# Second attention with its transpositions set among the attend products, and the down product's tiles in another order

## The chip, the cores and the metric

The kernel runs on one core of one Trainium2 chip. The metric is the device time of one execution in microseconds, as the median of the runs. Engines are named by the profile: PE is TensorE (matmuls and transpositions; PEld its weight loads), DVE is VectorE, ACT is ScalarE, POOL is GpSimd, SP is SyncE, which here only issues DMAs.

## What is computed

Two layers with residuals on x of shape (2, 512, 512): attention with 32 heads of 128, a gated feed-forward network, a second attention with 32 heads of 16, and a mixture of low-rank experts. The change lies at the end of the feed-forward network and in the second attention:

```python
def _L0_ffn_ref(x, ...):
    hidden = jax.nn.silu(x_flat @ gate_w.T) * (x_flat @ up_w.T)
    return hidden @ down_w.T                       # FF = 1792, H = 512
def _L1_attn_ref(x, w_qkv, b_qkv, w_out, b_out):   # N_HEADS = 32, hd = 16
    q, k, v = jnp.split(jnp.einsum('bsd,od->bso', x, w_qkv) + b_qkv, 3, axis=-1)
    scores = jnp.einsum('bqhd,bkhd->bhqk', q, k) * scale
    scores = scores + alibi[None, :, None, :]      # slope of the head * position
    scores = jnp.where(causal, scores, -1e9)
    attn = jax.nn.softmax(scores, axis=-1)
    out = jnp.einsum('bhqk,bkhd->bqhd', attn, v).reshape(B, S, D)
    return jnp.einsum('bsd,od->bso', out, w_out) + b_out
x = x + ffn(layernorm(x)); x = x + attn(layernorm(x)); x = x + experts(layernorm(x))
```

## The kernel before

x lies in eight tiles of 128 rows; tiles 0 to 3 are one batch, 4 to 7 the other. A product of two f32 operands is made of three matmuls on their rounded high and low halves (helper `product`, lines 64 to 66), each 128 x 128 by up to 512 columns. Every engine has its own hand-written program; they meet at semaphores only.

**Feed-forward, second half.** The down product of tiles 4 to 7 (`second_sequence`) sums 14 chunks of the hidden layer (`FC` = 14, three matmuls each) per tile in one PSUM bank. TensorE's order is: tile 4 whole; tile 5's first seven chunks; the transpositions of batch 0's normalised tiles (`norm.turn(0)`); tile 5's rest; the projection of the second attention's first query; tile 6's first half; the projection of keys; tile 7's first half; tile 6's rest; tile 7's rest; the projection of values. Each chunk of tile 7 counts `chunk_free`, from which GpSimd knows that memory of the hidden layer may be overwritten with the second attention's operands. VectorE scales each finished tile, adds it to x and takes its moments (`add_out`).

**Second attention.** Heads are taken in 4 chunks; a chunk is 8 heads for each of two batches, 16 units (batch, head), 64 units in all. Query and keys are projected for a whole chunk and batch, split in high and low halves (`split_operand`, VectorE, behind a rounding on ScalarE, `round_operand`), written out by SyncE (`a_spill_q`, `a_spill_k`) and read back by GpSimd (`read_back`) stacked by head in `stacked_q` and `stacked_k`, together with a block of slopes (`in_slope`), so that one matmul gives a score with its position term. A pick matrix and zeros are put in `stacked_q` first (`prepare`).

One step of TensorE (`step(c, s)`, line 1896) works on three units at once: it scores unit s + 3 (`score`, four matmuls of 128, 256, 384 and 512 columns into two banks, line 1828), turns the probabilities of unit s + 1 (`turn`, ten 128 x 128 transpositions in three groups of 4, 3 and 3, one PSUM bank each, line 1841), and attends unit s (`attend`, line 1853: four matmuls with the high halves of the turned probabilities, four with the low ones, 512, 384, 256 and 128 columns, all summed in one bank). Behind them stand, by the step's number, the turning of four gathered units, parts of the output product, and halves of the next projections (`project`), or `spread`.

VectorE per step: adds a projection's bias, masks the four scores of a unit and takes their maxima (`mask`, line 1992), takes the low half of the three turned groups (`split_turned`, line 2000). ScalarE per step (line 2156): exponentials of score tiles 0 and 1, casts of the three turned groups to the high half (`round_turned`, line 2132; its semaphore is `turned_hi`), in some steps one pass over values, spread values or the attended result, exponentials 2 and 3 (line 2123), the copy of the attended bank (`gather`, line 2140; `attend_read`), in some steps `round_operand`. The first attend of a unit waits for `attend_read` and for the low halves (`turned_split`); the first transposition waits for the four exponentials of its unit (`exp_done`).

At the start `step(-1, 13)` scores unit 0 behind the values' projection, once the pick has landed; then the values are spread and batch 1's normalised tiles turned (`norm.turn(1)`), and the loop begins at `step(-1, 14)`. Step 0 is the first with all three parts.

GpSimd's queue holds `read_back` with its waits, the splitting of weights and the addition of the output bias; SyncE's queue the loads of weights, the spills, and, behind the last spill, the loads of the experts' weights (`moe.fetch_down`, four of 512 KB).

## Time and profile before

| | |
|---|---|
| median of 3 runs | 1504.5 us (1502.46 to 1506.17) |
| the profiled execution | 1505.23 us, its span 1503.2 us |
| PE, PEld busy, share of the span | 95%, 80% |
| DVE, ACT, POOL busy | 67%, 57%, 37% |
| second attention, step 0 to step 52 | 1078.5 to 1334.2 us |

The table's shares are averages over stages with different limits. The prediction reads the stretch of the second attention by itself, then the order of time of an engine, in which each row is a run of like instructions with its start and duration; matmuls overlap, so a run's rate is read from the distance of starts. In brackets stands idle time ahead of a row and what ended it.

### The profile page before, as it was taken

The page shows a single profiled execution, that of the slowest core. Times are in us where ns is not written, and L with a number is a line of the kernel's source. Part 1 is how long each engine was busy: PE and PEld are TensorE (multiplying, and loading weights), DVE is VectorE, ACT ScalarE, POOL GpSimd, SP SyncE. Part 2 cuts the span into 40 slices and gives each one's busy share as a digit, 9 for nine tenths or more (in the row PEclk, how much of TensorE's full clock was granted, in tenths as well). Part 3 has the DMA queues.
Part 4 walks back from the last instruction along what each step waited for, and adds up shares of the span by engine and source line. Part 5 has one row for each costly group of instructions (what it writes and reads, how often), then busy time and mean ns, then how long its engine had stood idle before and what let it go on. Part 6 is the DMA issues. An engine that isn't in the chain of part 4 may idle for free.

```text
span 1503.2 us, 25443 instructions
## 1 busy us (share of the span) xinstructions
PE 1433.1 (95%) x7696; PEld 1195.1 (80%) x7696; DVE 1009.5 (67%) x2538; ACT 857.5 (57%) x2184; POOL 555.7 (37%) x484
## 2 busy tenths in 40 slices
PE   5899999999999999999988999999789999988999
PEld 4788888888888888888867888888567777776787
DVE  7776667766777667666656333344688889889742
ACT  2676566655566556665653332220589989988310
POOL 5474464644645456454240000023161314116500
PEclk9999999999999999999999999999899999999999
DMA  4010110100100001000021111114434435461000
GB/s 171 8 50 15 29 43 21 28 21 28 35 21 28 28 28 35 14 28 7 1 71 43 63 60 45 42 36 78 75 84 76 96 69 102 78 144 57 1 22 35
DMA packets 37517, 71.97 MB, mean 48 GB/s; under 512 B 4993, under 2 KB 5377, under 8 KB 36865
## 3 DMA queue, kind: packets, MB, share of 16 engines
q1 hardware_dynamic: 29664, 55.35, 11.8%
q0 software_dynamic: 7776, 15.73, 7.1%
q8 instruction: 33, 0.54, 0.2%
q14 instruction: 44, 0.35, 0.1%
HBM read 60.58 MB, written 10.49 MB: 47 GB/s over the span
## 4 chain that ended last, share of the span: by engine, by line
PE 80%; ACT 6%; DVE 6%; issue 4%; DMA 2%; POOL 1%; DVEq 0%; ACTq 0%; SPq 0%; POOLq 0%
PE ps_up L66 9%; PE ps_up L65 9%; PE ps_up L64 9%; PE ps_gate L64 8%; PE ps_gate L66 8%; PE ps_gate L65 8%; PE ps_out L64 5%; PE ps_out L66 5%; PE ps_out L65 5%; PE ps_out L556 4%; PE ps_up L1853 2%; ACT a_probs L2123 2%; PE ps_out L1841 2%; PE ps_gate L1828 2%; ACT a_probsT_hi L2132 2%
## 5 line engine op out<-in xcount | busy, mean ns | idle before, releaser
L822 ACT ACTIVATE a_probs<-a_probs,a_least 128x512 f32<-128x512 f32 (+3 forms) x256 | 143.0, 560 | 162.2 <-DVE a_least L683 157.2
L405 POOL TENSOR_TENSOR a_rotated<-a_by_cos,a_by_sin 128x512 f32<-128x512 f32 x80 | 103.7, 1296 | 224.9 <-DVE a_by_sin L706 222.7
L691 DVE TENSOR_TENSOR a_probsT_lo<-ps_out,a_probsT_hi 128x512 fp32r<-128x512 f32 (+3 forms) x256 | 118.5, 484 | 67.9 <-ACT a_probsT_hi L830 66.7
L830 ACT CAST a_probsT_hi<-ps_out 128x512 fp32r<-128x512 f32 (+3 forms) x256 | 101.5, 427 | 92.4 <-PE ps_out L556 91.6
L2123 ACT ACTIVATE a_probs<-a_probs,a_least 128x128 f32<-128x128 f32 (+3 forms) x256 | 142.2, 560 | 3.4 <-issue 1.6
L1992 DVE CUSTOM_DVE_ANT_0 a_probs<-ps_gate,a_causal 128x128 f32<-128x128 f32 (+3 forms) x256 | 117.1, 486 | 33.6 <-PE ps_gate L1828 20.7
L882 ACT ACTIVATE a_probs<-a_probs,a_inverse 128x128 f32<-128x128 f32 (+3 forms) x256 | 123.1, 553 | 9.6 <-DVE a_inverse L724 8.6
L415 POOL TENSOR_TENSOR a_query_lo<-a_rotated,a_query_hi 128x512 fp32r<-128x512 f32 x64 | 82.7, 1292 | 107.8 <-ACT a_query_hi L842 107.8
L683 DVE CUSTOM_DVE_ANT_0 a_probs<-ps_out,a_causal 128x512 f32<-128x512 f32 (+2 forms) x192 | 101.2, 551 | 29.6 <-PE ps_out L66 29.6
L64 PE MATMUL ps_up<-a_wo_hi,a_attended_hi 128*128 128x512 f32 x278 | 113.4, 408 | 2.3 <-issue 1.4
L64 PE MATMUL ps_gate<-xT_hi,a_wq_hi 128*128 128x512 f32 x256 | 108.9, 425 | 1.6 <-DVE a_values_lo L719 1.6
L2000 DVE TENSOR_TENSOR a_probsT_lo<-ps_out,a_probsT_hi 128x384 fp32r<-128x384 f32 (+1 forms) x192 | 108.8, 595 | 1.4 <-ACT a_probsT_hi L2132 1.2
L66 PE MATMUL ps_up<-a_wo_hi,a_attended_lo 128*128 128x512 f32 x278 | 108.9, 392 | 0.0
L65 PE MATMUL ps_up<-a_wo_lo,a_attended_hi 128*128 128x512 f32 x278 | 108.7, 391 | 0.0
L556 PE MATMUL ps_out<-ident,a_probs 128*128 128x128 f32 x640 | 102.5, 275 | 2.5 <-ACT a_probs L882 2.5
L66 PE MATMUL ps_gate<-xT_hi,a_wq_lo 128*128 128x512 f32 x256 | 100.6, 393 | 0.0
L65 PE MATMUL ps_gate<-xT_lo,a_wq_hi 128*128 128x512 f32 x256 | 100.1, 391 | 0.0
L2132 ACT CAST a_probsT_hi<-ps_out 128x384 fp32r<-128x384 f32 (+1 forms) x192 | 85.9, 512 | 22.6 <-PE ps_out L1841 22.0
L1828 PE MATMUL ps_gate<-a_stacked_k,a_stacked_q 128*128 128x128 f32 (+3 forms) x256 | 76.0, 374 | 21.9 <-DVE a_least L1992 13.4
L1841 PE MATMUL ps_out<-ident,a_probs 128*128 128x128 f32 x640 | 91.5, 274 | 5.2 <-ACT a_probs L2123 4.3
L713 DVE TENSOR_TENSOR x<-ps_up,x 128x512 f32<-128x512 f32 x64 | 44.2, 691 | 77.3 <-PE ps_up L66 77.3
L556 PEld LDWEIGHTS ps_out<-ident,a_probs 128*128 128x128 f32 x640 | 80.6, 142 | 13.8 <-ACT a_probs L882 3.0
(279 smaller groups left out, 4082.5 us busy)
## 6 DMA issues: line engine op xcount, KB each, us to landing
a_raw<-in_wq SPq DMA_DIRECT2D x36, 256.0 KB, 2.7
a_raw<-in_wo SPq DMA_DIRECT2D x36, 256.0 KB, 2.6
a_stacked_q<-a_spill_q POOLq DMA_DIRECT2D x48, 128.0 KB, 4.5
a_stacked_k<-a_spill_k POOLq DMA_DIRECT2D x24, 256.0 KB, 4.6
f_raw<-in_gate SPq DMA_DIRECT2D x14, 256.0 KB, 2.7
f_raw<-in_up SPq DMA_DIRECT2D x14, 256.0 KB, 2.9
f_raw<-in_down SPq DMA_DIRECT2D x14, 256.0 KB, 3.5
a_raw<-in_wk SPq DMA_DIRECT2D x12, 256.0 KB, 2.8
```

The costliest lines, as they stand in the source:

```text
L64: nc.tensor.matmul(out, left[0], right[0], start=start, stop=False)
L65: nc.tensor.matmul(out, left[0], right[1], start=False, stop=False)
L66: return nc.tensor.matmul(out, left[1], right[0], start=False, stop=stop)
L556: last = nc.tensor.transpose(ps_turn[:, t % 2, (i - t) * P:(i - t + 1) * P], probs[:, u % 2, at:at + P], m.ident[:])
L691: nc.vector.tensor_tensor(probsT[1][:, t % 2, 0:w], ps_turn[:, t % 2, 0:w], probsT[0][:, t % 2, 0:w].bitcast(F32), ALU.subtract).then_inc( ...
L822: nc.scalar.activation(tile, tile, ACT.Exp, bias=least[:, slot, i:i + 1], scale=-1.0, accum_out=total[:, slot, i:i + 1]).then_inc(exp_done, 1)
L882: nc.scalar.activation(tile, tile, ACT.Copy, scale=inverse[:, slot, i:i + 1]).then_inc(probs_ready, 1)
L1841: last = nc.tensor.transpose(ps_turn[:, t, to:to + P], probs[:, u % 4, at:at + P], m.ident[:])
L1992: nc.vector.tensor_tensor_reduce(out=probs[:, u % 4, at:at + w], in0=ps_score[:, i % 2, 0:w], in1=causal[:, SEQ - w:SEQ], scale=-float(HD1 ...
L2000: nc.vector.tensor_tensor(probsT[1][:, u % 2, at], ps_turn[:, t, 0:TURNED_WIDTH[t]], probsT[0][:, u % 2, at].bitcast(F32), ALU.subtract).t ...
L2123: nc.scalar.activation(tile, tile, ACT.Exp, bias=least[:, u % 4, i:i + 1], scale=-1.0, accum_out=total[:, u // 4 % 2, i, u % 4:u % 4 + 1]) ...
L2132: nc.scalar.copy(probsT[0][:, u % 2, at], ps_turn[:, t, 0:TURNED_WIDTH[t]]).then_inc(turned_hi, 1)
```

## The change

It has five parts. (1) In `step` the ten transpositions, eight attends and four scores no longer stand in blocks but one by one among each other; `attend` waits for `turned_hi` ahead of the four high products and for `turned_split` ahead of the four low ones. (2) The down product's order: first halves of tiles 4, 5 and 6, `norm.turn(0)`, first half of tile 7, then the rests with the query's and keys' projections between; the first unit is scored in the middle of tile 7's second half; values' projection, `spread` and `norm.turn(1)` follow it. (3) VectorE adds tiles 4 and 5 behind the keys' split, masks unit 0, then adds tiles 6 and 7; the query's `split_operand` in the last two steps ahead of step 0 comes one step later. (4) GpSimd issues the slopes ahead of the wait for the spilled keys (`fetch_slope`) instead of behind the keys. (5) SyncE waits for all keys read back (`stacked_k_in`) before it loads the experts' first weights. `least` and `total` move to another place in memory.

```diff
-    least = at("least", [P, 4, QT], DOWN_S_AT + 1056)
-    total = at("total", [P, 2, QT, 4], DOWN_S_AT + 1120)
+    least = at("least", [P, 4, QT], SMALL_AT + 256)
+    total = at("total", [P, 2, QT, 4], SMALL_AT + 320)
...
     def read_back(pool, c, s):
...
         else:
+            if not (isinstance(c, int) and c < 0):
+                fetch_slope(pool, c, s)
+            wait(pool, keys_out, 2 * 16 * (p + 1))
+            pool.sem_inc(wait_passed_pool, 1)
             for place, part in enumerate((0, 1, 0)):
...
-            pool.dma_start(stacked_k[96:P, b]..., dram["slope"][c if s < 8 else c + 1]).then_inc(stacked_k_in, 16)
+    def fetch_slope(pool, c, s):
+        pool.sem_inc(wait_passed_pool, 1)
+        pool.dma_start(stacked_k[96:P, batch_of(s)]..., dram["slope"][c if s < 8 else c + 1]).then_inc(stacked_k_in, 16)
...
         sp.wait_ge(keys_out, 2 * 16 * 2 * CHUNKS1)
+        sp.wait_ge(stacked_k_in, 16 * DMAS_K * 2 * CHUNKS1)
         moe.fetch_down(sp, (0, 1))
...
         prepare(0)
+        pool.wait_ge(ffn.chunk_free, 5)
+        fetch_slope(pool, -1, 8)
         read_back(pool, -1, 6)
-        pool.wait_ge(ffn.chunk_free, 5)
         read_back(pool, -1, 8)
...
         def attend(attending, part, k):
...
+            if k == 0:
+                if part == 0:
+                    if j == 0:
+                        wait(pe, side_read, side_count(cu, 3) if b else side_count(cu - 1, 11))
+                    wait(pe, attend_read, n)
+                    wait(pe, turned_hi, 3 * n + 3)
+                else:
+                    wait(pe, turned_split, 3 * n + 3)
...
         ffn.tensor(pe, bank_read, reads)
-        ffn.second_sequence(pe, 4, range(FC))
-        ffn.second_sequence(pe, 5, range(half))
+        for t in (4, 5, 6):
+            ffn.second_sequence(pe, t, range(half))
         norm.turn(pe, 0)
-        ffn.second_sequence(pe, 5, range(half, FC))
+        ffn.second_sequence(pe, 7, range(half))
         norm.ready(pe, 0)
         project(-1, 6, [0, 1])
-        ffn.second_sequence(pe, 6, range(half))
+        ffn.second_sequence(pe, 4, range(half, half + 3))
         project(-1, 8, [0, 1])
-        ffn.second_sequence(pe, 7, range(half))
+        ffn.second_sequence(pe, 4, range(half + 3, FC))
+        ffn.second_sequence(pe, 5, range(half, FC))
         ffn.second_sequence(pe, 6, range(half, FC))
-        ffn.second_sequence(pe, 7, range(half, FC))
+        pe.wait_ge(pick_in[0], 16)
+        pe.wait_ge(ffn.out_scaled, 6)
+        score((0, 0), 0)
+        score((0, 0), 1)
+        ffn.second_sequence(pe, 7, range(half, half + 4))
+        score((0, 0), 2)
+        score((0, 0), 3)
+        ffn.second_sequence(pe, 7, range(half + 4, FC))
         project(-1, 10, [0, 1])
+        spread(-1, 11)
+        norm.turn(pe, 1)

         def step(c, s):
             scoring, turning, attending = unit(c, s, 3), unit(c, s, 1), unit(c, s, 0)
-            turn 0; turn 1; score 0, 1; turn 2; attend 0; score 2, 3; attend 1
+            turn(turning, 0, [0, 1])
+            attend(attending, 0, 0)
+            score(scoring, 0)
+            attend(attending, 0, 1)
+            score(scoring, 1)
+            turn(turning, 0, [2])
+            attend(attending, 0, 2)
+            turn(turning, 0, [3])
+            attend(attending, 0, 3)
+            attend(attending, 1, 0)
+            turn(turning, 1, [0])
+            attend(attending, 1, 1)
+            turn(turning, 1, [1])
+            attend(attending, 1, 2)
+            turn(turning, 1, [2])
+            attend(attending, 1, 3)
+            turn(turning, 2, [0, 1, 2])
+            score(scoring, 2)
+            score(scoring, 3)
...
-        pe.wait_ge(pick_in[0], 16)
-        pe.wait_ge(ffn.out_scaled, 6)
-        step(-1, 13)
-        spread(-1, 11)
-        norm.turn(pe, 1)
         pe.wait_ge(pick_in[1], 16)
         each_chunk(pe, step)
...
     VectorE:
-        ffn.add_out(dve, 4)
-        ffn.add_out(dve, 5)
...
-            if side1 in ("query", "keys") and isinstance(c1, int) and c1 < 0:
+            if side1 in ("query", "keys") and isinstance(c1, int) and c1 < 0 and s1 < STEPS1 - 2:
                 split_operand(c1, s1)
-            if side2 in ("query", "keys") and not (isinstance(c2, int) and c2 < 0):
+            if side2 in ("query", "keys") and not (isinstance(c2, int) and c2 < 0 and s2 < STEPS1 - 2):
                 split_operand(c2, s2)
...
         step(-1, 9)
+        ffn.add_out(dve, 4)
+        ffn.add_out(dve, 5)
+        dve.wait_ge(causal_in, 16)
+        dve.wait_ge(ffn.chunk_free, 9)
+        step(-1, 13)
         ffn.add_out(dve, 6)
         ffn.add_out(dve, 7)
         norm.shift(dve, 1)
-        dve.wait_ge(causal_in, 16)
-        step(-1, 13)
```

On TensorE, one step before (`L1841` is `turn`, `L1828` `score`, `L1853` `attend`) begins so:

```order
L1841 MATMUL ps_out<-ident,a_probs 128x128 [waits a1_turned_split,a1_exp_done]
L1841 MATMUL ps_out<-ident,a_probs 128x128 x3
L1841 MATMUL ps_out<-ident,a_probs 128x128 [waits a1_turned_split]
L1841 MATMUL ps_out<-ident,a_probs 128x128 x2
L1828 MATMUL ps_gate<-a_stacked_k,a_stacked_q 128x128 [waits a1_score_masked]
L1828 MATMUL ps_gate<-a_stacked_k,a_stacked_q 128x256 [waits a1_score_masked]
L1841 MATMUL ps_out<-ident,a_probs 128x128 [waits a1_turned_split]
L1841 MATMUL ps_out<-ident,a_probs 128x128 x2
L1853 MATMUL ps_up<-a_probsT_hi,a_values 32x512 [waits a1_turned_split,a1_attend_read]
L1853 MATMUL ps_up<-a_probsT_hi,a_values 32x384
L1853 MATMUL ps_up<-a_probsT_hi,a_values 32x256
L1853 MATMUL ps_up<-a_probsT_hi,a_values 32x128
```

Behind these stand scores 2 and 3 and the four attends with the low half. The same step of the changed kernel (`L1857` is `turn`, `L1875` `attend`, `L1839` `score`):

```order
L1857 MATMUL ps_out<-ident,a_probs 128x128 [waits a1_turned_split,a1_exp_done]
L1857 MATMUL ps_out<-ident,a_probs 128x128
L1875 MATMUL ps_up<-a_probsT_hi,a_values 32x512 [waits a1_turned_hi,a1_attend_read]
L1839 MATMUL ps_gate<-a_stacked_k,a_stacked_q 128x128 [waits a1_score_masked]
L1875 MATMUL ps_up<-a_probsT_hi,a_values 32x384
L1839 MATMUL ps_gate<-a_stacked_k,a_stacked_q 128x256 [waits a1_score_masked]
L1857 MATMUL ps_out<-ident,a_probs 128x128
L1875 MATMUL ps_up<-a_probsT_hi,a_values 32x256
L1857 MATMUL ps_out<-ident,a_probs 128x128
L1875 MATMUL ps_up<-a_probsT_hi,a_values 32x128
L1875 MATMUL ps_up<-a_probsT_lo,a_values 32x512 [waits a1_turned_split]
L1857 MATMUL ps_out<-ident,a_probs 128x128 [waits a1_turned_split]
```

The first attend moves from behind ten transpositions to behind two, with another semaphore; eight transpositions come behind it. What follows is attend and transposition by turns, the third group of transpositions in a row, and scores 2 and 3 last.

On TensorE ahead of the loop, the first unit's scores before stand behind the values' projection (`a_wv`) and ahead of `spread` and `norm.turn(1)` (`L179`):

```order
L65 MATMUL ps_out<-xT_lo,a_wv_hi 128x512
L66 MATMUL ps_out<-xT_hi,a_wv_lo 128x512
L1828 MATMUL ps_gate<-a_stacked_k,a_stacked_q 128x128 [waits a1_stacked_q_in,a1_stacked_k_in,f0_out_scaled,a1_pick_in0]
L1828 MATMUL ps_gate<-a_stacked_k,a_stacked_q 128x256
L1828 MATMUL ps_gate<-a_stacked_k,a_stacked_q 128x384 [waits a1_score_masked]
L1828 MATMUL ps_gate<-a_stacked_k,a_stacked_q 128x512 [waits a1_score_masked]
L1793 MATMUL ps_out<-ident,a_values_turned 128x128 [waits a1_side_read]
L1793 MATMUL ps_out<-ident,a_values_turned 128x128 x3
L179 MATMUL ps_up<-ident,f_hidden 128x128 [waits ln_lo_done,ln_normal_done]
```

In the changed kernel they stand within the down product (`f_chunks`), the first two ahead of the first four of tile 7's last seven chunks:

```order
L65 MATMUL ps_up<-f_chunks 128x512
L66 MATMUL ps_up<-f_chunks 128x512
L1839 MATMUL ps_gate<-a_stacked_k,a_stacked_q 128x128 [waits a1_stacked_q_in,a1_stacked_k_in,f0_out_scaled,a1_pick_in0]
L1839 MATMUL ps_gate<-a_stacked_k,a_stacked_q 128x256
L64 MATMUL ps_up<-f_chunks 128x512
L65 MATMUL ps_up<-f_chunks 128x512
L66 MATMUL ps_up<-f_chunks 128x512
```

The first scores pass 33 products, 21 of tile 7 and 12 of the values' projection, and the scores of 384 and 512 columns stand four chunks behind the first two.

On SyncE behind the last spill of keys (`L1659`), before:

```order
L1659 DMA a_spill_k<-a_keys_hi 128x512 [waits a1_operand_split,a1_stacked_k_in]
L1659 DMA a_spill_k<-a_keys_lo 128x512
L1666 DMA a_raw<-in_wo 128x512 [waits a1_piece_split]
L1205 DMA moe_down_raw_5140<-in_down 128x1024 [waits a1_keys_out,a1_query_out]
L1205 DMA moe_down_raw_5141<-in_down 128x1024
L1205 DMA moe_down_raw_5142<-in_down 128x1024 [waits a1_side_made]
L1205 DMA moe_down_raw_5143<-in_down 128x1024
L1209 DMA moe_router_raw<-in_router 128x256
```

And in the changed kernel (`L1665` is the spill):

```order
L1665 DMA a_spill_k<-a_keys_hi 128x512 [waits a1_operand_split,a1_stacked_k_in]
L1665 DMA a_spill_k<-a_keys_lo 128x512
L1672 DMA a_raw<-in_wo 128x512 [waits a1_piece_split]
L1205 DMA moe_down_raw_5140<-in_down 128x1024 [waits a1_stacked_k_in,a1_keys_out,a1_query_out]
L1205 DMA moe_down_raw_5141<-in_down 128x1024
L1205 DMA moe_down_raw_5142<-in_down 128x1024 [waits a1_side_made]
L1205 DMA moe_down_raw_5143<-in_down 128x1024
L1209 DMA moe_router_raw<-in_router 128x256
```

The four loads of `in_down` keep their place, but the first waits for one thing more, the keys read back by GpSimd, and so do all behind it.

## Rows read from the trace of the kernel before

**Rows 1.** Windows, 52 steps: us, then PE, PEld, DVE, ACT, POOL busy

```profile
1078.70:1334.20 255.50, 244.35 (x1543) 193.64 (x1541) 225.63 (x669) 229.63 (x652) 76.07 (x102) 0.99 0.46 92
```

**Rows 2.** Timeline, PE before step 0: start, us, line, operation [idle <- releaser]

```profile
1057.91 0.47 PE L1828 MATMUL ps_gate<-a_stacked_k,a_stacked_q 128*128 128x128 f32 x2 [3.89 <-DMA a_stacked_k<-in_slope]
...
1061.54 1.97 PE L179 MATMUL ps_up<-ident,f_hidden 128*128 128x128 f32 x8 [0.77 <-DVE f_hidden L124]
...
1075.05 1.11 PE L1828 MATMUL ps_gate<-a_stacked_k,a_stacked_q 128*128 128x384 f32 x2 [3.32 <-DVE a_least L1992]
...
1078.52 1.11 PE L1841 MATMUL ps_out<-ident,a_probs 128*128 128x128 f32 x7
```

**Rows 3.** Timeline of PE, the last steps

```profile
1334.17 0.98 PE L1841 MATMUL ps_out<-ident,a_probs 128*128 128x128 f32 x7
...
1343.94 0.47 PE L1828 MATMUL ps_gate<-a_stacked_k,a_stacked_q 128*128 128x128 f32 x2 [3.93 <-issue]
...
1383.46 1.38 PE L1841 MATMUL ps_out<-ident,a_probs 128*128 128x128 f32 x10 [0.89 <-DVE a_probsT_lo L2000]
```

**Rows 4.** Timeline of PE, one step inside the attention

```profile
1207.16 0.93 PE L1841 MATMUL ps_out<-ident,a_probs 128*128 128x128 f32 x7
...
1208.16 0.49 PE L1841 MATMUL ps_out<-ident,a_probs 128*128 128x128 f32 x3
1208.41 0.83 PE L1853 MATMUL ps_up<-a_probsT_hi,a_values 128*32 128x512 f32 x4
...
1209.53 0.75 PE L1853 MATMUL ps_up<-a_probsT_lo,a_values 128*32 128x512 f32 x4
1210.11 0.44 PE L64 MATMUL ps_out<-xT_hi,a_wv_hi 128*128 128x512 f32 x1
```

**Rows 5.** Timeline of PE, first attention, a lone transposition

```profile
307.11 0.27 PE L556 MATMUL ps_out<-ident,a_probs 128*128 128x128 f32 x1
...
307.45 0.40 PE L65 MATMUL ps_gate<-xT_lo,a_wq_hi 128*128 128x512 f32 x1
307.68 0.39 PE L66 MATMUL ps_gate<-xT_hi,a_wq_lo 128*128 128x512 f32 x1
```

**Rows 6.** Timeline of ACT, end of one step

```profile
1353.38 1.32 ACT L2132 CAST a_probsT_hi<-ps_out 128x512 fp32r<-128x512 f32 x3
1354.59 0.63 ACT L2123 ACTIVATE a_probs<-a_probs,a_least 128x384 f32<-128x384 f32 x1
...
1355.20 0.71 ACT L2123 ACTIVATE a_probs<-a_probs,a_least 128x512 f32<-128x512 f32 x1
...
1356.03 0.57 ACT L2140 COPY a_gathered<-ps_up 32x512 f32<-32x512 f32 x1
```

**Rows 7.** Timeline of PE, start of the step behind it

```profile
1356.06 0.99 PE L1841 MATMUL ps_out<-ident,a_probs 128*128 128x128 f32 x7 [0.75 <-ACT a_probs L2123]
```

**Rows 8.** Timeline of ACT, a step with the result's rounding

```profile
1327.47 0.71 ACT L2145 ACTIVATE a_attended_hi<-ps_up,a_value_bias 128x512 fp32r<-128x512 f32 x1
1328.05 0.64 ACT L2123 ACTIVATE a_probs<-a_probs,a_least 128x384 f32<-128x384 f32 x1
```

**Rows 9.** Timeline of POOL ahead of step 0

```profile
1038.70 0.66 POOL L1748 DMA_DIRECT2D a_stacked_q<-in_pick  x1 [27.23 <-PE ps_up L66]
...
1047.39 1.62 POOL L1631 DMA_DIRECT2D a_stacked_k<-a_spill_k  x3 [0.80 <-issue]
```

**Rows 10.** Chain that ended last, before step 0: start, us, what

```profile
1039.65 6.94 DMA a_spill_k<-a_keys_lo
```

**Rows 11.** Page, part 6: DMA issues, count, KB each, us to landing

```profile
a_stacked_k<-a_spill_k POOLq DMA_DIRECT2D x24, 256.0 KB, 4.6
```

**Rows 12.** Timeline of DVE, one tile's addition and moments

```profile
1051.34 0.69 DVE L1078 TENSOR_TENSOR f_hidden<-ps_up,f_down_s 128x512 f32<-128x512 f32 x1 [2.40 <-PE ps_up L66]
...
1053.74 0.17 DVE L109 TENSOR_SCALAR ln_shifted<-moments 128x4 f32<-128x4 f32 x1
```

**Rows 13.** Timeline of SP, late in the attention

```profile
1329.10 2.14 SPq L1205 DMA_DIRECT2D moe_down_raw<-in_down  x4
```

More of the change, by code:

```diff
@@ L1829, in score, with turn @@
                              stacked_k[:, b, j // 2, 0:P * (i + 1)], start=True, stop=True).then_inc(score_made, 1)
[L1831 removed]
+        def turn(turning, t, blocks):
+            if not turning:
+                return
+            cu, u = turning
             n = STEPS1 * cu + u
[L1834 to L1842 removed]
@@ L1844, in attend @@
[L1844 to L1858 removed]
+            if 0 in blocks:
+                if t == 0:
+                    wait(pe, exp_done, 4 * n + 4)
+                wait(pe, turned_split, 3 * n - 2 + t)
@@ new lines, in turn, with attend @@
+            of_tile = [(k, i) for k in ((t,) if t < 2 else (2, 3)) for i in range(k, QT)]
+            for block in blocks:
+                k, i = of_tile[block]
+                at = SCORE_AT[i] + k * P
+                to = KEY_AT[k] - TURNED_AT[t] + (i - k) * P
+                mm = nc.tensor.transpose(ps_turn[:, t, to:to + P], probs[:, u % 4, at:at + P], m.ident[:])
+                if block == len(of_tile) - 1:
+                    mm.then_inc(turned, 1)
+        def attend(attending, part, k):
+            if not attending:
+                return
+            cu, u = attending
+            n, b, j = STEPS1 * cu + u, u // HPC, u % HPC
+            if k == 0:
[6 more added lines that the diff above has]
+                    wait(pe, turned_split, 3 * n + 3)
+            mm = nc.tensor.matmul(
+                ps_attend[0:2 * HD1, k * P:SEQ], values[:, b, k, j].rearrange("p h d -> p (h d)"),
+                probsT[part][:, u % 2, KEY_AT[k]:KEY_AT[k] + SEQ - k * P],
+                start=part == 0 and k == 0, stop=part == 1 and k == QT - 1)
+            if part == 1 and k == QT - 1:
+                mm.then_inc(attend_made, 1)
```

51 lines of the change are left out of this document (8 added, 43 removed).

## The prediction

> **What bounds the kernel now.** I read the stretches first, then the order of time of single steps, then the waits. In the second attention (52 steps, 1078.5 to 1334.2) TensorE is busy 244.35 of 255.5 us, ScalarE 229.63 and VectorE 225.63 [rows 1]: per step 4.70, 4.42 and 4.34 us against a step of 255.65 / 52 = 4.92 (first transposition at 1078.52 [rows 2] to that at 1334.17 [rows 3]). So TensorE's row sets the step, with the two others only 10% behind it; whatever lengthens a chain through ScalarE matters at once. Ahead of that stretch TensorE stands still for 3.89 us at the first score and 3.32 us at a later one [rows 2]; behind it, 3.93 us at 1343.94 [rows 3].
>
> **What interleaving changes on TensorE.** One step before: 7 transpositions, 2 scores, 3 transpositions, 4 attends, 2 scores, 4 attends, in 1210.11 - 1207.16 = 2.95 us [rows 4]. The four widths (512, 384, 256, 128 columns) take 1210.11 - 1209.53 = 0.58. A transposition costs 0.11: with one between wide products, the second product behind it comes 307.45 - 307.11 = 0.34 after it, of which 0.23 are the 512 columns (307.68 - 307.45) [rows 5]. So 10 x 0.11 + 3 x 0.58 = 2.84 (the scores have the four widths too): 0.11 per step is lost where a 128-column weight load follows a narrow product, and some 0.05 more at the first projection behind the last attend, an estimate from the same cause. In the new order no such load follows a narrow product but in the last three transpositions. TensorE's own gain is 0.11 to 0.16 us a step, 6 to 8 us over 52. A single transposition gets no cheaper: the lone one already costs what one in a row does (0.93 for seven, the last one's whole length included [rows 4]).
>
> The Trainium skill ("TensorE: Matmul & The Clock Gate", LDWEIGHTS) has a load of P columns take P / 1.2 ns, 107 ns for 128, and its section "Back-to-back issue gap" gives 128 moving columns some 56 ns. By that a row of transpositions is bound by its loads, and setting seven of ten among attends would hide 7 x 51 ns = 0.36 us a step. The trace speaks against it: 0.11 for a lone one [rows 5].
>
> **The chain that gets longer.** ScalarE's order is not touched: two exponentials, three casts of the turned tiles, exponentials 3 and 4, the copy `gather` of the attended bank, next step. The attend of the next unit writes the same bank, so it waits for that copy. Before, the attend stood 1208.41 - 1207.16 = 1.25 us behind the step's start, and the third group of transpositions ended 1208.16 + 0.49 - 1207.16 = 1.49 in [rows 4]. Now the first attend stands behind two transpositions (0.22), and from it to the last transposition stand 8 attends (1.16), 7 transpositions (0.77) and two scores (0.17): 2.10. From one first attend to the next: 2.10 + 0.27 (its own length [rows 5]) + 0.40 (a cast, a third of 1354.59 - 1353.38) + 0.61 (exponential 3, to 1355.20) + 0.83 (exponential 4, to the copy at 1356.03) + 0.57 (copy) [rows 6] + 0.05 to release = 4.83 us. The other branch, exponential 4 to the next transposition, is 1356.06 - 1355.20 = 0.86 [rows 6, 7] plus 0.22, under 1.45, so the copy ends last. This closes on itself: no step can be shorter, and long steps are not paid back by short ones. Before, the same links make 1.49 - 1.25 + 0.40 + 1.21 + 0.61 + 0.86 = 3.3, under every step.
>
> In three of eight steps one more ScalarE operation lies between the casts and exponential 3 (attended 1328.05 - 1327.47 = 0.58 [rows 8]; values and spread, one 512-column pass each, taken alike). So eight steps take at least 8 x 4.83 + 3 x 0.58 = 40.4, 5.05 each. Above that stands what the loop doesn't cover: the steps with the division and with both projection halves, where VectorE and TensorE are late anyway. TensorE's idle time in the stretch, 255.5 - 244.35 = 11.15 or 0.21 a step [rows 1], bounds it: 0 to 0.21. I take 0.13, nearer the upper end, since masks 3 and 4 and the third split now also wait behind the late casts on VectorE. Step 5.18, times 52 = 269.4, against 255.65: **+13.7 us** (5.05: +7; 5.26: +17.9).
>
> **The start.** Tile 7's first half now comes behind the normalised tile's transpositions, 22 groups of three products ahead of its old place: 66 x 0.23 = 15 us. So GpSimd's pick (0.5 MB) and memset, at 1038.70 before [rows 9], come at about 1023.6 and are gone when the keys are spilled; the keys' projection itself moves ahead by 12 products, 2.7 us. Before, the spill left at 1039.65 and took 6.94 beside the pick [rows 10]. After: it leaves at 1036.9 and lands in 4.6, as a read back of its kind does [rows 11], at best and 6.94 at worst; 0.3 to 0.8 to GpSimd's first read back, 1.1 to the issue of the third (1.62 for three [rows 9]), 4.6 to land: ready at 1048 to 1050. TensorE reaches the first score 33 products (7.6 us) before 1057.91 - 3.89 = 1054.0 [rows 2], at 1046.4. So the wait of 3.89 is down to 1.5 or a little more, and the unit's scores and masks lie beside tile 7's second half. Tile 7 ends near 1053; one tile's addition and moments take VectorE 1053.74 - 1051.34 = 2.40 [rows 12], so the first normalised tile is turned at about 1057 instead of 1061.54 [rows 2]: -4.5. The clock isn't lowered by such a wait: eight transpositions took 1.97 there [rows 2], seven take 0.93 in the loop [rows 4], which gives 1.3 on the sixteen (as if the second eight were partly hidden). Then the wait of 3.32 goes: the mask stood behind `split_operand`, which waited for ScalarE; it is now a step later. The two scores and six projection products behind that wait took 1078.52 - 1075.05 = 3.47 [rows 2], at 0.23 each 1.8: together -4.9. Sum **-11 us** up to step 0; bounds -8 (the wait of 1057.91 stays half) and -12.
>
> **The end.** The four `moe_down` loads went out at 1329.10 [rows 13], beside the last read back of keys, and TensorE waited 3.93 us for it [rows 3]. SyncE now waits for the keys. What is queued behind that wait are these loads and the router's, nothing else; they land some 7 us later than before, and their first user is GpSimd behind its split of `wo`. The slopes go ahead too, one transfer less behind the keys. That gives 3.9 back. But the last ten steps have few projections: they took 1383.46 - 1334.17 = 49.3 us with this wait [rows 3], 45.4 without, and at 4.83 plus two extra ScalarE passes they take 49.5 to 52. With the last attend behind the same copy: **+2.5 us** (0 to +4).
>
> Nothing: `least` and `total` elsewhere in memory; `turned_hi` for the first four attends (the split of the lower halves ends before their partners come); two more semaphore increments of GpSimd.
>
> **Sum.** 1505.2 (profiled) - 11 + 13.7 + 2.5 = 1510.4; the median of the three runs is 0.7 below the profiled one, so 1509.7, **1510**.
>
> **Rivals.** (a) The loop isn't binding, because some link is shorter than I read it: then TensorE's 0.16 a step comes through, and 1504.5 - 11 - 3.9 - 8 to -11 = about **1479**. For it: TensorE is still the busiest. Against it: ScalarE already held TensorE back at 1356.06, with 0.75 idle [rows 7]. (b) Transpositions are hidden by attends: 0.05 of the 0.11 of each of the seven goes, 0.36 a step, which shortens the loop by as much, to 4.47: 1504.5 - 11 - 3.9 with 52 x (4.92 - 4.7) = -11 and some -3 from the last ten steps, about **1475**. That is what the Trainium skill's rule quoted above would give. (c) The loop binds, but nothing is added to it: 5.05 a step, -11 + 7 + 1 = **1502**, no measurable difference. (d) Slower still: the keys land late. If spill and read back meet other transfers again they are there at 1051 to 1052, TensorE stands 5 us with tile 7 unfinished, and the clock falls as it did after the 3.89 us [rows 2]. Then the 21 down products run at about twice 0.23, which costs some 2 more; the start gains 4 instead of 11: **1517**. It decides from a landing later than about 1050.
>
> **Chances.** The forecast (1502 to 1518) 0.62, (a) 0.12, (b) 0.04, (c) 0.12, (d) 0.10. Within 0.3% (4.5 us, about what a measurement of this kernel can tell from no change) is 1500 to 1509. The forecast's case lies above it in some 0.38, in it in 0.21, below in 0.03. Slower 0.48, within 0.33, faster 0.19. The range takes both ends of the three terms: -12 + 7 + 0 = -5, -8 + 17.9 + 4 = +14, so 1499 to 1518; it leaves out (a) and (b).
>
> **What would show it.** Steps of 4.83 or more with TensorE idle before the first attend (ended by the copy) or the first transposition (by an exponential), ScalarE idle before the casts; steps of 5.3 to 5.5 where an extra pass lies on ScalarE. First transposition of step 0 near 1067.5, no wait over 2 us at the first score, none at 1340, the clock near 1 throughout. Wrong if short steps stay at 4.3 (then (a)), if 10 transpositions among attends add less than 0.9 us (then (b)), or if the first score waits more than 3 us (then (d)).

## The result and the profile after

| | before | changed |
|---|---|---|
| median of 3 runs | 1504.5 us (1502.46 to 1506.17) | 1521.2 us (1517.79 to 1521.76) |
| ratio of changed to before | | 1.0102 (95% interval 1.0075 to 1.0128) |
| span of the profiled execution | 1503.2 us | 1519.2 us |

The change makes the kernel 1% slower. The prediction had the sign, but said 1510 with an upper end of 1518, below what was measured. The spans differ by 16.0 us. I cut both traces at landmarks of TensorE that both programs have: the first transposition of batch 0's normalised tiles, that of batch 1's, the first transpositions of steps 0, 52 and 62, and the first transposition of the experts' normalised tiles. (This table and those below are worked out from the starts of those matmuls in each trace.)

| stretch, us | before | changed | difference | predicted |
|---|---|---|---|---|
| span's start to batch 0's transpositions | 1020.14 | 1023.02 | +2.9 | 0 |
| to batch 1's transpositions | 41.40 | 39.49 | -1.9 | -4.5 |
| to step 0 | 16.97 | 12.98 | -4.0 | -6.2 |
| 52 steps | 255.65 | 269.74 | +14.1 | +13.7 |
| steps 52 to 61 | 49.29 | 51.28 | +2.0 | +2.5 with the next row |
| last step to the experts' transpositions | 5.44 | 7.17 | +1.7 | |
| the experts | 114.27 | 115.47 | +1.2 | 0 |

The first row is no effect of the change: the down product's first matmul, which stands ahead of everything that was moved, already starts at 1008.60 instead of 1005.72. In the eleven other profiled kernels of this study the stretch took between 1018.9 and 1022.8 us.

The 52 steps as one window of the changed kernel (us, then busy time and instructions of PE, PEld, DVE, ACT, POOL, mean clock, DMA share, GB/s), to be read against [rows 1]:

```profile
1075.50:1345.20 269.70, 246.42 (x1541) 198.06 (x1541) 230.59 (x674) 237.18 (x657) 76.36 (x102) 1.00 0.47 88
```

TensorE is idle for 269.70 - 246.42 = 23.3 us there instead of 11.15. Of the 14.2 us by which the window is longer, 12.1 are idle time of TensorE and 2.1 busy time: its waits grew. The timeline of TensorE at two step starts (27 and 28) shows them:

```profile
1215.05 0.43 PE L1857 MATMUL ps_out<-ident,a_probs 128*128 128x128 f32 x2 [0.77 <-ACT a_probs L2155]
1215.64 0.42 PE L1875 MATMUL ps_up<-a_probsT_hi,a_values 128*32 128x512 f32 x1 [0.16 <-ACT a_gathered L2172]
...
1217.56 0.49 PE L1857 MATMUL ps_out<-ident,a_probs 128*128 128x128 f32 x3
...
1220.49 0.43 PE L1857 MATMUL ps_out<-ident,a_probs 128*128 128x128 f32 x2 [0.72 <-ACT a_probs L2155]
1221.09 0.41 PE L1875 MATMUL ps_up<-a_probsT_hi,a_values 128*32 128x512 f32 x1 [0.16 <-ACT a_gathered L2172]
...
1225.27 0.50 PE L64 MATMUL ps_out<-a_wo_hi,a_attended_hi 128*128 128x512 f32 x1 [0.94 <-DVE a_values L2094]
```

The same step on ScalarE, from one copy of the attended bank to the next:

```profile
1214.94 0.57 ACT L2172 COPY a_gathered<-ps_up 32x512 f32<-32x512 f32 x1
...
1216.79 0.59 ACT L2164 CAST a_probsT_hi<-ps_out 128x512 fp32r<-128x512 f32 x1 [0.26 <-PE ps_out L1857]
1217.70 0.87 ACT L2164 CAST a_probsT_hi<-ps_out 128x384 fp32r<-128x384 f32 x2 [0.33 <-PE ps_out L1857]
1218.46 0.59 ACT L2199 COPY a_values_turned<-ps_out 128x512 f32<-128x512 f32 x1
1218.94 0.63 ACT L2155 ACTIVATE a_probs<-a_probs,a_least 128x384 f32<-128x384 f32 x1
...
1219.56 0.71 ACT L2155 ACTIVATE a_probs<-a_probs,a_least 128x512 f32<-128x512 f32 x1
...
1220.38 0.57 ACT L2172 COPY a_gathered<-ps_up 32x512 f32<-32x512 f32 x1
```

This is the predicted loop, closed: copy at 1214.94, attend at 1215.64, last transpositions at 1217.56, casts to 1218.46, one more pass, exponentials 3 and 4, copy at 1220.38. It takes 5.44 us; the prediction had 4.83 + 0.58 = 5.41 for a step with an extra pass.

Ahead of step 0, TensorE of the changed kernel, against [rows 2]:

```profile
1051.75 0.47 PE L1839 MATMUL ps_gate<-a_stacked_k,a_stacked_q 128*128 128x128 f32 x2 [2.30 <-DMA a_stacked_k<-a_spill_k]
...
1062.02 0.66 PE L1801 MATMUL ps_out<-ident,a_values_turned 128*128 128x128 f32 x4 [1.85 <-ACT a_values_turned L2199]
1062.51 1.04 PE L179 MATMUL ps_up<-ident,f_hidden 128*128 128x128 f32 x8
...
1066.90 0.84 PE L1839 MATMUL ps_gate<-a_stacked_k,a_stacked_q 128*128 128x384 f32 x2 [2.25 <-DVE a_least L2021]
...
1068.23 0.63 PE L66 MATMUL ps_out<-xT_hi,a_wq_lo 128*128 128x512 f32 x1
1068.66 0.63 PE L64 MATMUL ps_out<-xT_hi,a_wq_hi 128*128 128x512 f32 x1
```

The wait of 3.89 us became 2.30, that of 3.32 us is gone, but waits of 1.85 and 2.25 us stand in between, where the kernel before waited 0.77 and 1.31. Behind them eight projection products come 0.43 us apart instead of 0.23.
### The profile page after: what moved, and what is told of

Read it like the earlier page. It is cut to its first block, busy times and chain, and to the rows that moved or that the text cites. A ratio compares the mean times of both kernels' runs of the same rounds, so it can differ in the third digit from the quotient of the medians.

```text
span 1519.2 us, 25451 instructions
## 1 busy us (share of the span) xinstructions
PE 1437.1 (95%) x7696; PEld 1201.7 (79%) x7696; DVE 1013.8 (67%) x2538; ACT 865.7 (57%) x2184; POOL 554.5 (37%) x484
## 4 chain that ended last, share of the span: by engine, by line
PE 82%; ACT 6%; DVE 5%; issue 2%; POOL 2%; DMA 2%; ACTq 0%; SPq 0%; DVEq 0%; POOLq 0%
PE ps_up L66 9%; PE ps_up L65 9%; PE ps_up L64 9%; PE ps_gate L64 8%; PE ps_gate L66 8%; PE ps_gate L65 8%; PE ps_up L1875 5%; PE ps_out L64 5%; PE ps_out L66 5%; PE ps_out L65 5%; PE ps_out L556 4%; PE ps_out L1857 4%; ACT a_probs L2155 2%; PE ps_gate L1839 2%; ACT a_gathered L2172 1%
## 5 line engine op out<-in xcount | busy, mean ns | idle before, releaser
L1857 PE MATMUL ps_out<-ident,a_probs 128*128 128x128 f32 x640 | 132.6, 276 | 20.1 <-ACT a_probs L2155 17.9
L2029 DVE TENSOR_TENSOR a_probsT_lo<-ps_out,a_probsT_hi 128x384 fp32r<-128x384 f32 (+1 forms) x192 | 112.7, 598 | 17.4 <-ACT a_probsT_hi L2164 12.6
L2164 ACT CAST a_probsT_hi<-ps_out 128x384 fp32r<-128x384 f32 (+1 forms) x192 | 93.0, 514 | 41.0 <-PE ps_out L1857 40.4
L1857 PEld LDWEIGHTS ps_out<-ident,a_probs 128*128 128x128 f32 x640 | 80.9, 142 | 36.4 <-ACT a_probs L2155 20.7
L556 PE MATMUL ps_out<-ident,a_probs 128*128 128x128 f32 x640 | 101.9, 274 | 2.5 <-ACT a_probs L882 2.5
L64 PE MATMUL ps_up<-a_probsT_hi,a_values_hi 128*128 128x512 f32 (+3 forms) x256 | 86.4, 337 | 4.8 <-DVE a_probsT_lo L691 4.7
```

The source lines that it names most:

```text
L64: nc.tensor.matmul(out, left[0], right[0], start=start, stop=False)
L556: last = nc.tensor.transpose(ps_turn[:, t % 2, (i - t) * P:(i - t + 1) * P], probs[:, u % 2, at:at + P], m.ident[:])
L1857: mm = nc.tensor.transpose(ps_turn[:, t, to:to + P], probs[:, u % 4, at:at + P], m.ident[:])
L2029: nc.vector.tensor_tensor(probsT[1][:, u % 2, at], ps_turn[:, t, 0:TURNED_WIDTH[t]], probsT[0][:, u % 2, at].bitcast(F32), ALU.subtract).t ...
```

## Experiments

Where a time is compared, it is with the kernel before on the same chip, run between (medians 1505.7 to 1506.5 us). Profiles give the place. Names used in the expectations: theory L is the loop above.

**Is it the step?** x1 takes the step's order back, x2 puts the new step alone into the kernel before.

```diff
 x1_old_step, against the changed kernel
-            turn(turning, 0, [0, 1])
-            attend(attending, 0, 0)
...
+            turn(turning, 0, [0, 1, 2, 3]); turn(turning, 1, [0, 1, 2])
+            score(scoring, 0); score(scoring, 1)
+            turn(turning, 2, [0, 1, 2])
+            for k in range(QT): attend(attending, 0, k)
+            score(scoring, 2); score(scoring, 3)
+            for k in range(QT): attend(attending, 1, k)
```

> The changed kernel with TensorE's step in the order of before (four and three transpositions, scores 0 and 1, three transpositions, four high attends, scores 2 and 3, four low attends); start, slopes and the late load of the experts' weights stay as changed. Theory L (the interleaved step is bound by a loop through ScalarE and the single attended bank): 52 steps take 255 to 257 us again instead of 269.7, the last ten some 45.5 instead of 51.3, and the tail loses its 3 us; with the start 6 us shorter than before that is 1494 to 1498. Rival S (the start or the later loads cost what was lost, not the step): 1515 to 1521.

Measured: 1500.73 us, ratio 0.9962 (0.9948 to 0.9976).

> The kernel before with the interleaved step alone. Theory L: 52 steps of 5.18, 269 to 271 us against 255.7 (+14), the wait of 3.9 us at the late load is still there but partly taken out of the same loop, the last ten steps 51 to 55: 1520 to 1525. Rival S: 1504 to 1508.

Measured: 1527.13 us, ratio 1.0145 (1.0126 to 1.0164), 2 us above what theory L gave and far from rival S. The 52 steps took 269.93 us as it said. The stretches ("to step 0" from batch 0's transpositions), with the mean length of a step by its place s in a round of eight (steps 8 to 51), for these and the next three kernels:

| | to step 0 | 52 steps | 52 to 61 | s=0 | 1 | 2 | 3 | 4 | 5 | 6 | 7 |
|---|---|---|---|---|---|---|---|---|---|---|---|
| before | 58.4 | 255.65 | 49.29 | 4.95 | 5.19 | 4.38 | 4.26 | 4.81 | 6.20 | 5.08 | 4.45 |
| changed | 52.5 | 269.74 | 51.28 | 5.24 | 5.02 | 5.18 | 5.42 | 5.61 | 5.56 | 4.91 | 4.60 |
| x1 | 52.9 | 260.08 | 45.78 | 4.92 | 5.20 | 4.39 | 4.25 | 4.81 | 6.38 | 5.08 | 4.43 |
| x2 | 57.8 | 269.93 | 53.55 | 5.24 | 5.02 | 5.18 | 5.42 | 5.61 | 5.57 | 4.91 | 4.60 |
| x3 | 52.9 | 260.69 | 47.96 | 5.18 | 4.90 | 4.69 | 5.00 | 5.19 | 5.61 | 4.97 | 4.27 |
| x4 | 54.2 | 266.65 | 48.98 | 5.24 | 5.06 | 4.90 | 5.22 | 5.60 | 5.58 | 4.91 | 4.33 |
| x5 | 52.8 | 251.95 | 44.92 | 4.95 | 5.16 | 4.39 | 4.25 | 4.81 | 6.26 | 5.09 | 4.43 |

The step is settled: x1 has the step lengths of before, x2 those of the changed kernel, and the 14 us go with it. It costs at s = 2, 3 and 4 (+0.80, +1.16, +0.80) and gives something back at s = 5 (-0.64).

x1 was expected at 1494 to 1498 and is slower. Its 52 steps took 260.08 instead of 255.65, and 3.0 of these 4.4 us are one step: step 5 takes 12.47 us, against 9.44 before and 6.89 in the changed kernel (0.8 more lie in step 6). GpSimd and VectorE of x1 there:

```profile
1093.79 9.92 POOL L1727 TENSOR_TENSOR x<-x,a_out_bias 128x512 f32<-128x512 f32 x8
...
1099.48 5.73 DVE L2041 TENSOR_TENSOR a_result<-a_summed,a_inverse 128x256 f32<-128x256 f32 x1
```

and what TensorE waits for:

```profile
1105.48 1.14 PE L1839 MATMUL ps_gate<-a_stacked_k,a_stacked_q 128*128 128x384 f32 x2 [5.66 <-DVE a_least L2013]
```

A product of 128 x 256 numbers that takes 0.42 us in most other places lasts 5.73. Whatever the start gained, this product ended at about the same time (1105.56 before, 1105.21 in x1), because GpSimd's eight additions of the output bias run where they ran: they stand in its queue behind the read back of keys (0, 0). That became theory G, tested below.

**Which links make the loop?** x3 shortens it on TensorE's side, x4 on ScalarE's.

```diff
 x3_third_group_early, against the changed kernel
             attend(attending, 0, 3)
-            attend(attending, 1, 0)
-            turn(turning, 1, [0])
...
+            turn(turning, 1, [0, 1, 2]); turn(turning, 2, [0, 1, 2])
+            for k in range(QT): attend(attending, 1, k)
             score(scoring, 2)
```

> The changed kernel with the six last transpositions in a row ahead of the four low attends: from the first attend to the last transposition 0.58 + 0.17 + 8 x 0.109 = 1.62 us instead of 2.10, so the loop is 4.35 instead of 4.83 us. Theory L: steps with no extra pass fall from 5.18 to some 4.8, the mean of 52 to 4.92 to 5.0, total 1505 to 1511. Rival T (a transposition or attend among the others costs TensorE more than one in a row): only three of seven are put back in a row, so at most three sevenths of the loss goes, 1515 or more.

Measured: 1506.74 us, ratio 1.0004 (0.9995 to 1.0013); the 52 steps took 260.69 us, 5.01 each, and 4.97 in steps 8 to 51. At s = 2, 3 and 4 the last transposition stands 1.55 to 1.61 us behind the first attend instead of 2.14 or 2.15, which is 0.54 to 0.59 less where 0.48 was worked out, and these steps fall by 0.49, 0.42 and 0.42. Rival T is out. Step 5 takes 9.69 us, because x3 reaches the product `a_result` early enough to wait for GpSimd again (3.98 us, theory G below).

```diff
 x4_short_exp, against the changed kernel
-            tile = probs[:, u % 4, SCORE_AT[i]:SCORE_AT[i + 1]]
+            tile = probs[:, u % 4, SCORE_AT[i] if i < 3 else SCORE_AT[i] + 256:SCORE_AT[i + 1]]
```

> The changed kernel with the fourth exponential of each unit over its last 256 of 512 columns only (the left 256 keys of the last query tile are left out of the computation). That pass takes 0.21 us less, and nothing else is changed. Theory L: the loop and with it each of some 62 steps is 0.21 shorter, 11 us over the 52 and 13 in all: 1507 to 1511. Rival T, or a step set by VectorE: 1518 to 1521.

Measured: 1513.59 us, ratio 1.0054 (1.0039 to 1.007), 7.6 us under the changed kernel where theory L said 13. By the traces even less is due to the steps: 3.1 us lie in the 52 steps and 2.3 in the last ten, while 4.1 lie ahead of the change, where nothing differs, and 1.7 came back at the start. Steps 53 to 58 do as expected (0.16 to 0.23 less each), and so do s = 2, 3 and 7 (-0.28, -0.20, -0.27). Step 5 is 1.6 us longer than in the changed kernel (`a_result` lasts 2.95 us instead of 2.39, and five products behind that wait are slow). The others don't move. So the loop through exponential 4 binds three places of eight. At s = 4 the wait that ends last is the 0.94 us for `a_values` in the timeline above: the cast of the spread values stands on ScalarE behind the late casts but ahead of exponential 4, VectorE takes the low half, and the output product behind it waits. x4 doesn't touch that chain, x3 does, and at s = 4 only x3 helps. I had this step in the sum as "TensorE and VectorE late anyway"; the loss there is from the same late casts by another way out.

**Is the start's gain given back at step 5?** x5 is x1 with one move in GpSimd's queue, x7 is the same move in the kernel before.

```diff
         def chunk(c):
             if first:
                 read_back(pool, c, 0)
-                add_out_bias()
...
         prepare(1)
+        add_out_bias()
         read_back(pool, -1, 14)
```

> x1_old_step with GpSimd's eight additions of the output bias moved from behind the read back of keys (0, 0) to ahead of the read back of the query (-1, 14), where GpSimd waits some 30 us. Theory G (what the start gained is given back at step 5, where VectorE's product a_result waits until GpSimd's run of additions has ended, 5.73 us in x1): step 5 falls from 12.47 to 6.2, step 6 from 5.15 to 4.4, and the whole to 1493 to 1495. Rival (a_result waits for something else, or the additions cost as much elsewhere): 1500 to 1502.

Measured: 1494.06 us, ratio 0.9923 (0.9907 to 0.994). Step 5 takes 5.63 us instead of 12.47, and the 52 steps 251.95.

> The kernel before with the bias additions moved in the same way. Theory G: step 5 falls from 9.44 to 6.2, 3.2 us less, 1502 to 1503.5 against 1506. Rival: no change.

Measured: 1503.01 us, ratio 0.9978 (0.9965 to 0.9992), and step 5 takes 5.79 us instead of 9.44. Theory G holds in both. In x7 the gain is in the median and in step 5 but hardly in the profiled execution, the second longest of the eleven (1505.53 us): its 52 steps took 255.13 against 255.65. There step 21 took 8.81 us instead of 6.23, with a wait of 1.48 us for keys read back, and an `a_result` of 1.43 us.

> The changed kernel as it is, interleaved step and all, with GpSimd's bias additions ahead of the read back of the query (-1, 14). In the changed kernel a_result lasts 2.39 us instead of 0.4, so at most 2 us of step 5 (6.89) go: 1518 to 1520 against 1521.2. If the interleaved step alone costs what x1 to x5 say, x11 minus x5 is 25 to 27 us.

Measured: 1519.07 us, ratio 1.0094 (1.0077 to 1.011). x11 and x5 differ in the step's order alone: 25.0 us. In their traces, whose spans differ by 21.3 because the stretch ahead of the change is 2.1 shorter in x11, 16.1 lie in the 52 steps (268.08 against 251.95), 6.5 in the last ten (51.38 against 44.92) and 1.1 at the last attend (6.56 against 5.43). Step 5 took 4.76 us instead of the changed kernel's 6.89, about the 2 us that were expected at most.

**Single parts of the change.** x8 takes only SyncE's wait ahead of the experts' loads into the kernel before.

```diff
         sp.wait_ge(keys_out, 2 * 16 * 2 * CHUNKS1)
+        sp.wait_ge(stacked_k_in, 16 * DMAS_K * 2 * CHUNKS1)
         moe.fetch_down(sp, (0, 1))
```

> The kernel before, and SyncE waits for all keys read back ahead of the experts' first weights. The wait of 3.93 us at 1343.94 goes, and some 0.5 comes back in the last steps as in x1 (49.29 to 45.78 there): 1502 to 1503 against 1506. Rival (the stall is not from these loads): 1506. If the later loads held up the experts, their part (114.3 us from their first transposition) would grow.

Measured: 1502.64 us, ratio 0.9976 (0.9965 to 0.9986). Steps 52 to 61 take 45.75 us instead of 49.29, the experts 114.27 as before. SyncE's loads move from 1329.10 [rows 13] to

```profile
1339.02 1.77 SPq L1205 DMA_DIRECT2D moe_down_raw<-in_down  x4
```

so this part is worth 3.5 us, and the experts don't miss the earlier loads.

x9 is x5 with the query's `split_operand` back in its place ahead of the masks.

```diff
-            if side1 in ("query", "keys") and isinstance(c1, int) and c1 < 0 and s1 < STEPS1 - 2:
+            if side1 in ("query", "keys") and isinstance(c1, int) and c1 < 0:
...
-            if side2 in ("query", "keys") and not (isinstance(c2, int) and c2 < 0 and s2 < STEPS1 - 2):
+            if side2 in ("query", "keys") and not (isinstance(c2, int) and c2 < 0):
```

> x5_old_step_bias_early with the query's split_operand of the last two steps ahead of step 0 back in its old place, ahead of the masks. If the wait of 3.32 us of the kernel before went by that move, it comes back here: 3.3 of wait and some 1.2 of slower products behind it, less what the query's earlier spill gives: 1497 to 1499 against 1494. Rival (the wait went because other work had moved): 1493.5 to 1494.5.

Measured: 1497.51 us, ratio 0.9945 (0.9929 to 0.9962). The wait is back, to the digit, in x9's timeline of TensorE, and the stretch from batch 1's transpositions to step 0 takes 17.00 us instead of 13.06:

```profile
1076.23 0.84 PE L1839 MATMUL ps_gate<-a_stacked_k,a_stacked_q 128*128 128x384 f32 x2 [3.32 <-DVE a_least L2013]
```

x6 is x5 with VectorE's addition of tile 6 ahead of the first masks.

```diff
         ffn.add_out(dve, 5)
+        ffn.add_out(dve, 6)
         dve.wait_ge(causal_in, 16)
         dve.wait_ge(ffn.chunk_free, 9)
         step(-1, 13)
-        ffn.add_out(dve, 6)
         ffn.add_out(dve, 7)
```

> x5_old_step_bias_early with VectorE's addition of tile 6 ahead of the first unit's masks instead of behind them. In the changed kernel VectorE stands idle for 6.7 us ahead of the masks while tile 6 is done, and then has two tiles to add behind them. Expected: the normalised tiles are turned 2.3 us earlier, total 1490.5 to 1493. Rival (the next wait, the values' spread or the masks of the next unit, takes its place): the same as x5.

Measured: 1493.97 us, ratio 0.9923 (0.9907 to 0.9939), no gain over x5. In its trace the wait ahead of the values' transpositions falls from 1.85 us to 0.68: that is what tile 6's place costs, 1.2 us and not the 2.3 that was expected. It didn't reach the end of this execution: the keys came later (TensorE waited 3.44 us at the first score, 2.56 in x5), and the eight slow products, which x5 has at the query's projection, stand here behind that wait, so that tile 7 itself was late:

```profile
1051.30 0.47 PE L1839 MATMUL ps_gate<-a_stacked_k,a_stacked_q 128*128 128x128 f32 x2 [3.44 <-DMA a_stacked_k<-a_spill_k]
...
1052.73 0.63 PE L64 MATMUL ps_up<-f_chunks 128*128 128x512 f32 x1
...
1061.99 0.66 PE L1801 MATMUL ps_out<-ident,a_values_turned 128*128 128x128 f32 x4 [0.68 <-ACT a_values_turned L2191]
```

From batch 0's transpositions to step 0 x6 took 52.5 us and x5 52.8. Another 1.1 us went at step 57 (4.95 against 3.87), where `a_result` lasts 1.54 us beside GpSimd's splitting of weights. Six kernels with the old step have such a long product there and a step of 4.9 to 5.0 (x1, x6 to x10); before and x5 have neither and take 3.87.

x10 is x5 with the attends in another order.

```diff
-            for k in range(QT): attend(attending, 0, k)
+            for k in (0, 1, 3, 2): attend(attending, 0, k)
...
-            for k in range(QT): attend(attending, 1, k)
+            for k in (0, 3, 2, 1): attend(attending, 1, k)
```

> x5_old_step_bias_early with the attends of a unit in the order 512, 384, 128, 256 columns (high) and 512, 128, 256, 384 (low), so that no 128-column weight load (score 2, the first projection product) follows a 128-column product. By the prediction's reading of rows 4 that is 0.08 us (1206.69 - 1206.03 = 0.66 for four widths instead of 0.58) and 0.05 us (0.28 instead of 0.23 behind the first projection product) a step: 62 x 0.08 to 0.13 = 5 to 8 us if all of it reached the end, 3 to 5 with the steps that wait for VectorE: 1489 to 1491. Rival (the loss is not from the narrow product): 1494.

Measured: 1493.33 us, ratio 0.9909 (0.9892 to 0.9927), too close to x5 to tell apart. The expected 1489 to 1491 was missed, and the rival's 1494 is nearer. Its steps at s = 2, 6 and 7 are 0.09 to 0.12 shorter (4.39, 5.09, 4.43 to 4.29, 4.97, 4.34), but those at s = 1 and 3 are 0.10 longer (5.16 and 4.25 to 5.26 and 4.35), and the others hardly move. The 52 steps went from 251.95 to 250.84, and the last ten from 44.92 to 46.46, of which 1.0 is step 57 again. So the TensorE time that interleaving was to win shows at three places of eight, about 0.1 us each, and almost none of it reaches the end.

## Why the prediction was wrong

**The loop: right, in mechanism and size.** Predicted 5.18 us a step and 269.4 for 52, measured 5.187 and 269.7. The loop closes at 5.44 where 5.41 was worked out. Two of its links had no row of their own: from the first attend to the last transposition 2.10 was added up and 2.14 to 2.20 measured at most places, and from the copy's end to the attend 0.05 was put in and 0.13 measured (1214.94 + 0.57 to 1215.64). The allowance of 0.13 for "what the loop doesn't cover" came out right for a partly wrong reason: x4 shows the loop through exponential 4 at three places of eight, and the largest loss outside it is the wait for `a_values` at s = 4, which I hadn't named. "No step can be shorter than 4.83" was wrong as worded: steps s = 7 take 4.60, because a step is measured from transposition to transposition and the loop runs from copy to copy (4.97 us there, 1194.37 to 1199.34 on ScalarE). From copy to copy the shortest distance is 4.79.

**The interleaving's own gain** was read as 0.11 to 0.16 us a step. x10, which takes the narrow products away without interleaving, gets 0.09 to 0.12 at three places. A transposition among attends costs what one in a row costs, as [rows 5] said: in step 28 two of them with an attend of 384 columns between are 0.28 us apart (1222.32 and 1222.60), and 384 columns take 0.17.

**The start: the failed step.** I took -11, and it was -5.9. These 5.1 us are the largest part of the 10.8 by which the spans' difference (16.0) missed the forecast (5.2); 2.9 lie ahead of the change, 2.4 behind the 52 steps, and 0.4 in them. Four terms of the start were off. First, VectorE: the sum took one tile's addition (2.40 us [rows 12]) behind tile 7, but in the changed order tiles 6 and 7 both stand behind the masks, as the order of VectorE shows. In the trace:

```profile
1053.79 0.29 DVE L2021 CUSTOM_DVE_ANT_0 a_probs<-ps_gate,a_causal 128x128 f32<-128x128 f32 x1 [6.70 <-PE ps_up L66]
...
1056.44 0.69 DVE L1078 TENSOR_TENSOR f_hidden<-ps_up,f_down_s 128x512 f32<-128x512 f32 x1
...
1058.72 0.66 DVE L1078 TENSOR_TENSOR f_hidden<-ps_up,f_down_s 128x512 f32<-128x512 f32 x1
...
1061.08 0.17 DVE L109 TENSOR_SCALAR ln_shifted<-moments 128x4 f32<-128x4 f32 x1
```

1061.08 - 1056.44 = 4.64 us for the two. Tile 7's last product ended near 1057.4, so the second tile kept tile 7 waiting for 1.2 us, which is also what x6 took from the wait behind it. Second, the first score waited 2.30 us instead of 1.5. Third, "the clock isn't lowered by such a wait": the transpositions did run at the full rate (1.04 for eight), but the clock fell 5 us later, behind two more waits, and slowed eight products by 0.2 each, 1.6 us. That is no chance of one execution: all nine profiled kernels with the changed start have such a stretch of seven to nine products, x6 and x10 behind the first score, x4 at both places. Fourth, the 1.7 us that the faster transpositions gained met a longer wait for masks (2.25 instead of 1.31), and 0.9 was left where 1.3 was taken. Together these are some 4 us; the last 1 us isn't traced to a term.

**What is behind step 0: not asked.** The prediction ended the start's account at step 0 and carried the gain to the end. It should have asked what else step 5 waits for. The row stood in the trace of before: the same product `a_result` took 3.1 us there. In the changed kernel little of this shows, because the slow steps arrive at step 5 almost as late as before; but it bounds what the start could have brought with any step: x1 gave back 3.8 us at steps 5 and 6 (12.47 and 5.15 against 9.44 and 4.38) of the 5.4 it had won.

**The end: under-sized.** The wait of 3.93 went as forecast (x8: 3.5 us), and the last ten steps grew by 2.0 in spite of it. Behind them came 2.9 us more, of which the forecast had at most a half: the last attend waits 2.68 us for the copy instead of 1.69, and in this trace the attends and the experts' first transpositions behind it run slowly, with a granted clock of 0.73 from 1400 to 1405:

```profile
1401.88 0.93 PE L1875 MATMUL ps_up<-a_probsT_hi,a_values 128*32 128x512 f32 x4 [2.68 <-ACT a_gathered L2172]
1402.62 1.27 PE L1875 MATMUL ps_up<-a_probsT_lo,a_values 128*32 128x512 f32 x4
1403.68 1.91 PE L179 MATMUL ps_gate<-ident,moe_normal 128*128 128x128 f32 x8
```

In the experts, 0.6 of the last 1.2 us are these slow transpositions (1.0, less a shorter wait behind them), and 0.6 a longer wait for `moe_ranksT_lo` at 1433.52 (1.29 instead of 0.64). x4 has both as well. x2 and x11 have the same step and the same wait of 2.68 ahead of the last attend, but the full clock behind it, and neither loss. So that wait alone doesn't explain the clock, and I have no cause for these 1.2 us.

**The stretch ahead of the change** gave the changed kernel's profile 2.9 us that are chance. It is in the comparison of the spans, and I can't say how much of it is in the medians; in the kernels run later, unchanged there, the stretch lies anywhere in 4 us.

**The range.** The three terms' ends were 7 + 0 and 17.9 + 4 around a start of -12 to -8. The loop was in its range; the start at -5.9 lay outside its own, because that range held only the uncertainty of the keys' landing and no chance that an engine's queue had been miscounted. With the start at -5.9 the same sum gives 1515, inside the range; the 6 us that are still missing are the 2.9 ahead of the change, the 2.4 at the end and smaller ones.

## What to carry to other kernels

A step that is bound by one engine with two others within 10% is a set of loops; before instructions are moved among each other, work out each loop through the shared buffer that they write (here one PSUM bank, freed by a copy that stands last on ScalarE), because spreading the producer's work over the step makes every one of its consumers late. Carry a gain at the start of a pipeline past its first fixed point: look in the queues of the idle engines for work that is pinned by another event, here GpSimd's bias additions behind a read back. The best kernels of this study, x5, x6 and x10 at 1493 to 1494 us, keep the changed start and the late loads, take back the interleaving and move those additions into a wait of GpSimd that lasted 30 us in x1.

## What the hardware showed

VectorE's `a_result` reads two SBUF tensors. Beside GpSimd's run of additions it isn't slowed by some share; it ends when GpSimd pauses. GpSimd in the changed kernel:

```profile
1096.88 6.22 POOL L1727 TENSOR_TENSOR x<-x,a_out_bias 128x512 f32<-128x512 f32 x5
1103.06 1.26 POOL L1718 TENSOR_TENSOR a_wq_hi<-a_raw,a_zeros 128x512 fp32r<-128x512 f32 x1
1104.40 1.35 POOL L1720 TENSOR_TENSOR a_wq_lo<-a_raw,a_wq_hi 128x512 fp32r<-128x512 f32 x1
```

and VectorE:

```profile
1102.21 2.39 DVE L2049 TENSOR_TENSOR a_result<-a_summed,a_inverse 128x256 f32<-128x256 f32 x1
```

The additions and the instruction behind them follow without a gap; the first gap lies between 1103.06 + 1.26 = 1104.32 and 1104.40, and `a_result` ends at 1104.60. In the kernel before that gap began at 1105.27 and the product ended at 1105.56, in x1 at 1104.92 and 1105.21, although the product had started 3.1 and 5.7 us earlier. VectorE's splits, which read one tensor from PSUM and one from SBUF, kept their length beside the same additions (two in 1.16 us in the kernel before, at 1098.10). The Trainium skill ("GPSIMD Engine Reference", Specifications) says that GpSimd's SBUF interfaces are shared with VectorE, with contention for VectorE instructions in a 2-port mode or with two SBUF inputs. The runs agree as to which instruction is hit; the size, 5.73 us for a product of 0.42, is theirs. In twelve of the thirteen traces the first `a_result` ends 0.28 or 0.29 us behind the last GpSimd instruction ahead of a gap of 0.07 or 0.08 us, wherever it started. That GpSimd's gap lets it through is an inference, and it isn't the whole rule: in the kernel before the last `a_result` (1393.61, 1.31 us) ends 0.29 us behind a GpSimd instruction (1393.34, 1.29 us) that the next one follows without a gap, and it is this next one that is long, 1.48 us instead of 1.27. In x5 a product that started together with a GpSimd instruction (both at 1350.44) took its 0.42 us, and GpSimd's took 1.57 instead of 1.28. Why the product gets in there and not between the additions no run shows.
